# One-core hybrid block, Mamba stage: another order of VectorE's work in the odd tiles

## The chip, the cores and the metric

The kernel runs on one core of a Trainium2 chip. The metric is device time in microseconds (us) of one execution. The Mamba stage, in which the change lies, takes about 590 us of it.

## The reference

The kernel computes one block on 2 x 1024 rows of 512 elements, fp32, with a residual addition after each part:

```
x = x + attention(layernorm(x))      # sliding window, 16 heads
x = x + moe(layernorm(x))            # 8 experts, top 2
x = x + mamba(layernorm(x))
x = x + moe(layernorm(x))            # the same weights
```

The part that matters here is mamba (16 heads of 64, state 128, blocks of 64 rows, so two blocks in a tile of 128 rows):

```
z, xBC, dt_raw = split(x @ in_proj_w.T)            # 1024, 1280, 16 columns
xBC = silu(conv4(xBC) + conv_b)                    # 4 taps along the rows
dt = softplus(dt_raw + dt_bias);  A = -exp(A_log)
X = x_heads * dt;  A_disc = dt * A
Y = Y_diag + Y_off                                 # in a block, and from the state before it
Y = Y + x_heads * D
y = Y * silu(z);  y = y / rms(y) * norm_w
return y @ out_proj_w.T
```

## The kernel before

Four stages run one after the other: attention, the experts (moe_a), Mamba, the experts again (moe_b). Each engine has one instruction stream, written out by hand, and waits on semaphores. What an engine does next is set by the order of the calls in the code alone.

In the function mamba, 16 tiles of 128 rows are worked off in 8 turns of two tiles. A turn i scans tiles 2i (even) and 2i+1 (odd), and, in its first seven turns (front), prepares the two tiles of the next turn: it normalises their rows, multiplies them by in_proj_w, and convolves the 10 channel groups in five units (0 to 4) of two groups each, 256 rows wide. Of a unit TensorE makes the product (channels), ScalarE copies it into cin and makes the last tap (conv_in), VectorE adds the other three taps in six instructions (convolve, L1696), and ScalarE applies silu (conv_out, L1927).

For an odd tile VectorE does, in this order before the change: mask_products (L1731), scale_rows (L1737, waits for xs from ScalarE), keep_factors, convolve 1, mean_of, rest_of_y (L1711, the low half of the y of the tile before), convolve 2, mix (L1748, decays times cb), first_block (L1755, state in the middle of the tile), time_steps (L1660 to L1675, softplus by a series, 16 small instructions), second_block (L1762, state at the tile's end), convolve 3, put_out (L1725, the output with its residual, for the even tile t-1), scored.statistics (L201 to L204), own_out (L1772), scored.normalise (L215), convolve 4, rows_done (L1779, L1782, L1784) and logits_out (L246).

What the other engines need of it:

- TensorE: own_rows waits for mix and first_block; from_states (L2186) for second_block; scored.turn (L226) for scored.normalise; the turning of y (L2149) of the next tile for rows_done. Its order near the odd tile's end is own_rows, channels 4, from_states, gate_rows half 0 (L2119), scored.turn (L226), gate_rows half 1 (L2119), scored.product (L238), and then the next even tile: scan_rows (L2131 to L2136), turn_xs (L2142), turn_y (L2149).
- ScalarE: behind the exponentials (L1991) come conv_out 0, conv_out 1, conv_in 3, conv_out 2, conv_out 3, conv_in 4, conv_out 4, scored.turned_out (L232, which scored.product waits for), gate, and the next tile's exp table and small_out (L1947).
- GpSimd (step): xlast (L1592), mean_power (L1585), mid (L1602), xskip (L1606), and after first_block the product for the state (L1610), which second_block waits for.

```
                scored.turned_out(act, t - 1, bank[7])   # ScalarE, behind conv_out(n, 4, 1 - pp)
                gate_rows(t + 1, 0, 1, cin_ready, UNITS * n + 5)   # TensorE, behind scored.turn
                scored.product(pe, t - 1, bank[7])
```

Of the kernel before, what the change touches and what calls it, by code (L numbers as in the profile page):

```python
# [81 lines left out]
def after(eng, sem, n):  # L82

    if not isinstance(n, int) or n > 0:
        eng.wait_ge(sem, n)
# [15 lines left out]
def spread(ap, axis, n):  # L101

    v = ap.unsqueeze(axis)
    shape = list(v.shape)
    shape[axis] = n
    return v.broadcast_to(shape)
# [1287 lines left out]
def mamba(core, x_in, x_out, xn_rows, out_w, conv_w, conv_b, a_log, d_skip, dt_bias, norm_w):  # L1394
# [74 lines left out]
    with stage_semaphores(nc, "mam") as sem, ExitStack() as ctx:  # L1469
# [160 lines left out]
        def _(dve):  # L1630
            def statistics(link, n, par, turn):
                dve.wait_ge(x_loaded[par], 16 * turn + 16)
                link(nc.vector.bn_stats(st[:, par], x[:, par]))
                nc.vector.nop(nofuse=True)
                link(nc.vector.bn_aggr(mv[:, par], st[:, par]))
                nc.vector.tensor_scalar(var_eps[:, par:par + 1], mv[:, par, 1:2], EPS, None, ALU.add).then_inc(var_ready, 1)
# [20 lines left out]
            def time_steps(link, n, pp):  # L1657

                dve.wait_ge(e_mag_ready, n + 1)
                link(nc.vector.tensor_scalar(ratio, e_mag, 2.0, None, ALU.add))  # L1660
                link(nc.vector.reciprocal(ratio, ratio))
                link(nc.vector.tensor_tensor(ratio, e_mag, ratio, ALU.mult))
                link(nc.vector.tensor_tensor(ratio2, ratio, ratio, ALU.mult))
                link(nc.vector.tensor_scalar(series, ratio2, 1.0 / 15, None, ALU.mult))
                for odd in (13, 11, 9, 7, 5, 3):
                    link(nc.vector.scalar_tensor_tensor(out=series, in0=series, scalar=1.0 / odd, in1=ratio2,
                                                        op0=ALU.add, op1=ALU.mult))
                link(nc.vector.scalar_tensor_tensor(out=series, in0=series, scalar=1.0, in1=ratio,
                                                    op0=ALU.add, op1=ALU.mult))
                link(nc.vector.tensor_scalar(u, u, 0.0, None, ALU.max))  # L1670
                link(nc.vector.scalar_tensor_tensor(out=dt[:, pp], in0=series, scalar=2.0, in1=u,
                                                    op0=ALU.mult, op1=ALU.add))
                for par in range(2):
                    wide = da_wide[:, 2 * pp + par].rearrange("p (r s h) -> p r s h", r=REPS, s=2)
                    last = nc.vector.tensor_tensor(wide, spread(spread(dt[:, pp, par * H:par * H + H], 1, 2), 1, REPS),  # L1675
                                                   spread(a_pair, 1, REPS), ALU.mult)
                last.then_inc(da_ready, 1)

            def first_factor(i):

                return core.keep[:, i % TURNS_PER_BATCH:i % TURNS_PER_BATCH + 1]

            def halo_in(n):
                dve.wait_ge(cin_ready, UNITS * n)
                nc.vector.tensor_scalar(cin[:, :, 0:halo], cin[:, :, PAIR:PAIR + halo], first_factor(n), None, ALU.mult)\
                    .then_inc(halo_ready, 1)

            def convolve(link, n, unit):

                dve.wait_ge(cin_ready, UNITS * n + unit + 1)  # L1690
                if unit == 0:
                    after(dve, halo_ready, n)
                slot = conv[unit % 3]
                for k in range(halo):
                    for j, c in enumerate(units[unit]):
                        last = nc.vector.scalar_tensor_tensor(out=slot[:, j], in0=cin[:, c, k:k + PAIR],  # L1696
                                                              scalar=taps[:, c, k:k + 1], in1=slot[:, j],
                                                              op0=ALU.mult, op1=ALU.add)
                    if k < halo - 1:
                        link(last)  # L1700
                last.then_inc(conv_ready, 1)

            def mean_of(t):
                dve.wait_ge(squares_ready, t + 1)
                nc.vector.tensor_scalar(mean_eps, squares, 1.0 / INNER, EPS, ALU.mult, ALU.add).then_inc(mean_ready, 1)
# [22 lines left out]
            def mask_products(t):  # L1728
                dve.wait_ge(held_ready, t + 1)
                after(dve, mixed_ready, t)  # L1730
                nc.vector.tensor_tensor(cb, held[:, BC:BC + BLK], core.upto[:], ALU.mult).then_inc(cb_ready, 1)  # L1731

            def scale_rows(t, pp, par):
                dve.wait_ge(xs_ready, 2 * t + 2)
                after(dve, yd_made, 2 * t)
                after(dve, xlast_ready, t)
                nc.vector.tensor_tensor(by_head(xdt), by_head(xs), spread(dt[:, pp, par * H:par * H + H], 2, MHD), ALU.mult)\  # L1737
                    .then_inc(xdt_ready, 1)

            def keep_factors(t, keep):  # L1740
                dve.wait_ge(exps_ready, t + 1)
                after(dve, mid_decayed, t)
                nc.vector.tensor_scalar(kept, exps[:, KEPT:KEPT + H], keep, None, ALU.mult).then_inc(kept_ready, 1)
# [42 lines left out]
            def turn(link, i, pp, first=False, front=True):  # L1786
                n = i + 1
                t = 2 * i
                mask_products(t)
                scale_rows(t, pp, 0)  # L1790
                keep_factors(t, first_factor(i))
                if front:
                    halo_in(n)
                    for par in range(2):
                        statistics(link, t + 2 + par, par, n)
                if not first:
                    mean_of(t - 1)
                    rest_of_y(t - 1)
                if front:
                    for par in range(2):  # L1800
                        normalise(t + 2 + par, par)
                mix(t)
                first_block(t)
                second_block(t)
                if first:
                    rest_of_w_out()
                if not first:
                    put_out(t - 1)
                    dve.wait_ge(added, t)
                    scored.statistics(dve, link, xres)  # L1810
                if front:
                    for par in range(2):
                        rest_out(t + 2 + par, par)
                own_out(t)
                if not first:
                    dve.wait_ge(out_made, t)
                    scored.normalise(dve, t - 1, xres)
                rows_done(link, t, 0)
                if front:
                    magnitudes(link, n)  # L1820
                if front:
                    convolve(link, n, 0)
                if not first:
                    scored.logits_out(dve, t - 1, bank[7])
                t = 2 * i + 1
                mask_products(t)
                scale_rows(t, pp, 1)
                keep_factors(t, core.ones[:, 0:1])
                if front:
                    convolve(link, n, 1)  # L1830
                mean_of(t - 1)
                rest_of_y(t - 1)
                if front:
                    convolve(link, n, 2)
                mix(t)
                first_block(t)
                if front:
                    time_steps(link, n, 1 - pp)
                second_block(t)
                if front:  # L1840
                    convolve(link, n, 3)
                else:
                    dve.wait_ge(z_made, 2 * TILES)
                    sort.early_choice(link)
                put_out(t - 1)
                dve.wait_ge(added, t)
                scored.statistics(dve, link, xres)
                own_out(t)
                dve.wait_ge(out_made, t)
                scored.normalise(dve, t - 1, xres)  # L1850
                if front:
                    convolve(link, n, 4)
                rows_done(link, t, 1)
                scored.logits_out(dve, t - 1, bank[7])

            link = Chain(dve, chain)
# [18 lines left out]
            for i in range(TURNS):  # L1875
                turn(link, i, i % 2, first=(i == 0), front=(i < LAST))
# [486 lines left out]
```

## Time and profile before

| | us |
|---|---|
| runs, median of 3 | 1661.57 |
| runs, lowest and highest | 1661.12, 1667.22 |
| the profiled execution, its own time | 1657.97 |
| its span in the trace | 1656.3 |
| busy in the span: TensorE, VectorE, ScalarE, GpSimd | 1509.8, 927.4, 720.9, 596.1 |

The profiled execution lies 3.6 us below the median of the runs, and its span 1.67 us below its own time. Times in the trace are from the span's start. A row of the timeline is a run of like instructions on one engine: start, duration, what it is, how many, and in brackets the idle time before it and what ended that. The Mamba stage lies between about 750 and 1350 us.

### The profile page before, as it was taken

The page shows a single profiled execution, that of the slowest core. Times are in us where ns is not written, and L with a number is a line of the kernel's source. Part 1 is how long each engine was busy: PE and PEld are TensorE (multiplying, and loading weights), DVE is VectorE, ACT ScalarE, POOL GpSimd, SP SyncE. Part 2 cuts the span into 40 slices and gives each one's busy share as a digit, 9 for nine tenths or more (in the row PEclk, how much of TensorE's full clock was granted, in tenths as well). Part 3 has the DMA queues.
Part 4 walks back from the last instruction along what each step waited for, and adds up shares of the span by engine and source line. Part 5 has one row for each costly group of instructions (what it writes and reads, how often), then busy time and mean ns, then how long its engine had stood idle before and what let it go on. Part 6 is the DMA issues. An engine that isn't in the chain of part 4 may idle for free. (4 is left out here: it accounts for less than half of the span.)

```text
span 1656.3 us, 34129 instructions
## 1 busy us (share of the span) xinstructions
PE 1509.8 (91%) x11983; PEld 1267.9 (77%) x12004; DVE 927.4 (56%) x2133; ACT 720.9 (44%) x1784; POOL 596.1 (36%) x473
## 2 busy tenths in 40 slices
PE   6999999998699999978789999999999869999997
PEld 5788788787498889966668677777777648898896
DVE  4677777776622234215787786977878662222222
ACT  3666666666032234225454445554445302222222
POOL 5556556555223334430232222233222403333342
PEclk9999999999799999989899999999999979999999
DMA  5356455444589777432001101010010037787753
GB/s 211 117 184 207 143 183 204 160 163 160 200 274 320 204 229 195 84 61 75 14 20 33 39 27 40 20 33 23 34 37 21 20 140 249 209 265 199 185 91 56
DMA packets 95917, 212.36 MB, mean 128 GB/s; under 512 B 7216, under 2 KB 7216, under 8 KB 94512
## 3 DMA queue, kind: packets, MB, share of 16 engines
q1 hardware_dynamic: 76736, 166.58, 28.8%
q0 software_dynamic: 17472, 40.90, 12.4%
q10 hardware_dynamic: 1584, 3.15, 0.5%
q8 instruction: 86, 1.41, 0.3%
q14 instruction: 39, 0.32, 0.1%
HBM read 136.94 MB, written 73.66 MB: 127 GB/s over the span
## 5 line engine op out<-in xcount | busy, mean ns | idle before, releaser
L1298 PE MATMUL bank<-ring,halves 128*128 x1872 | 332.1, 326 | 3.5 <-ACT halves L1137 3.5
L1298 PEld LDWEIGHTS bank<-ring,halves 128*128 128x128 f32 x1872 | 303.0, 188 | 10.8 <-issue 4.5
L498 POOL TENSOR_TENSOR arena<-arena 128x1024 f32<-128x1024 f32 x64 | 123.8, 1934 | 142.1 <-DVE arena L578 140.6
L1696 DVE SCALAR_TENSOR_TENSOR arena<-arena 128x256 f32<-128x256 f32 x240 | 136.8, 612 | 17.8 <-ACT arena L1916 15.0
L1147 ACT ACTIVATE arena<-bank 128x512 f32<-128x512 f32 x78 | 46.7, 598 | 204.4 <-PE bank L1329 73.4
L1592 POOL TENSOR_TENSOR arena<-arena 128x1024 f32<-128x1024 f32 x16 | 31.3, 1958 | 273.6 <-ACT arena L1970 235.1
L791 PE MATMUL bank<-arena 128*128 128x128 f32 x1024 | 124.8, 281 | 1.8 <-ACT arena L691 0.8
L710 ACT ACTIVATE arena<-arena 128x256 f32<-128x256 f32 x256 | 126.2, 499 | 0.0
L791 PEld LDWEIGHTS bank<-arena 128*128 128x128 f32 x1024 | 118.8, 194 | 7.7 <-issue 3.6
L1117 POOL DMA_INDIRECT out_dram<-arena x39 | 61.8, 1584 | 153.4 <-issue 87.9
L1117 POOL DMA_INDIRECT mid_rows<-arena x39 | 61.8, 1585 | 151.7 <-issue 92.0
L1109 POOL DMA_INDIRECT arena<-normalised_rows,arena x78 | 79.4, 1018 | 99.3 <-PE bank L1281 47.6
L1137 ACT ACTIVATE halves<-bank 128x512 fp32r<-128x512 f32 x78 | 46.7, 598 | 147.1 <-PE bank L1281 147.0
L1186 DVE TENSOR_TENSOR moe_b_act_rest<-bank,moe_b_act_high 128x384 fp32r<-128x384 f32 x39 | 21.8, 558 | 152.3 <-ACT moe_b_act_high L1152 152.3
L2088 PE MATMUL bank<-halves,w_in_high 128*128 128x256 f32 x640 | 91.9, 286 | 1.6 <-DVE halves L1646 1.6
L1186 DVE TENSOR_TENSOR moe_a_act_rest<-bank,moe_a_act_high 128x384 fp32r<-128x384 f32 x39 | 21.7, 556 | 125.4 <-ACT moe_a_act_high L1152 125.4
L1927 ACT ACTIVATE arena<-arena 128x256 f32<-128x256 f32 x80 | 35.6, 501 | 115.3 <-DVE arena L1696 115.2
L2088 PEld LDWEIGHTS bank<-halves,w_in_high 128*128 128x128 f32 x640 | 80.9, 188 | 2.8 <-DVE halves L1646 1.8
L1191 DVE TENSOR_TENSOR halves<-bank,halves 128x512 fp32r<-128x512 f32 x78 | 53.9, 692 | 47.1 <-ACT halves L1137 47.0
L1180 DVE SCALAR_TENSOR_TENSOR arena<-arena,bank 128x352 f32<-128x352 f32 x78 | 45.2, 579 | 55.3 <-PE bank L1298 52.6
L2119 PE MATMUL bank<-w_in_high,halves 128*128 128x512 f32 x256 | 73.1, 431 | 1.0 <-ACT arena L1916 1.0
L831 PE MATMUL bank<-ident,arena 128*128 128x128 f32 x512 | 69.2, 279 | 2.7 <-POOL arena L498 2.7
(285 smaller groups left out, 3293.6 us busy)
## 6 DMA issues: line engine op xcount, KB each, us to landing
ring<-expert_halves SPq DMA_DIRECT2D x16, 4352.0 KB, 18.7
expert_halves<-expert_high SPq DMA_DIRECT2D x16, 1088.0 KB, 8.4
expert_halves<-expert_rest SPq DMA_DIRECT2D x16, 1088.0 KB, 10.5
arena<-in_w_dram SPq DMA_DIRECT2D x8, 1088.0 KB, 6.7
normalised_rows<-arena SPq DMA_DIRECT2D x33, 256.0 KB, 2.0
arena<-in_x_dram SPq DMA_DIRECT2D x32, 256.0 KB, 2.8
arena<-mid_rows SPq DMA_DIRECT2D x32, 256.0 KB, 2.8
w_in_raw<-in_in_w_dram SPq DMA_DIRECT2D x16, 290.0 KB, 7.1
```

What stands on the lines that cost most here:

```text
L498: nc.gpsimd.tensor_tensor(held, held, spread(rinv[:, HG * g:HG * g + HG], 2, 2 * P), ALU.mult)\
L710: last = nc.scalar.activation(held, held, ACT.Exp, scale=-1.0, bias=nmax[:, h:h + 1], accum_out=psum_p[:, h:h + 1])
L791: last = nc.tensor.matmul(proj[:, c * P:c * P + P], wqkv[:, k, first + c * P:first + c * P + P], xnT[:, k], start=(k == 0), stop=(k == KD ...
L831: last = nc.tensor.transpose(b[:, j * P:j * P + P], probs[:, g // 2, HG * (g % 2) + 2 * half + j // 2, (j % 2) * P:(j % 2 + 1) * P], core. ...
L1109: nc.gpsimd.indirect_dma_start(out=rows[:, s % 2], out_offset=None, in_=xn_rows, in_offset=bass.IndirectOffsetOnAxis(ap=index[:, s:s + 1], ...
L1117: nc.gpsimd.indirect_dma_start(out=x_rows, out_offset=bass.IndirectOffsetOnAxis(ap=index[:, s:s + 1], axis=0), in_=y[:, s % 2], in_offset= ...
L1137: nc.scalar.activation(rows_parts[0][:, par], bank[0][:], ACT.Copy).then_inc(rows_high, 1)
L1191: nc.vector.tensor_tensor(rows_parts[1][:, par], bank[0][:], rows_parts[0][:, par], ALU.subtract)\
L1298: last = nc.tensor.matmul(bank[1 + 2 * par + part][:, 0:INTER], rows_parts[a][:, par, k * P:k * P + P], weights(at, b, (2 * k + part) * IN ...
L1696: last = nc.vector.scalar_tensor_tensor(out=slot[:, j], in0=cin[:, c, k:k + PAIR], scalar=taps[:, c, k:k + 1], in1=slot[:, j], op0=ALU.mul ...
L2088: last = nc.tensor.matmul(unit_banks[unit][:, j * PAIR:(j + 1) * PAIR], w_parts[b][:, k, at:at + P], x_parts[a][:, k], start=((a, b, k) == ...
L2119: last = nc.tensor.matmul(b_out[:], x_parts[a][:, k, par * P:par * P + P], w_parts[b][:, k, half * 512:half * 512 + 512], start=((a, b, k) ...
```

## The change

In the odd tile's part of VectorE's turn, mix and first_block are called ahead of convolve 2, and time_steps moves from behind first_block to behind scored.normalise, so that second_block, convolve 3, put_out, the statistics, own_out and normalise all run ahead of it. Nothing is added or removed, and no other engine's stream changes. It takes effect where front holds, in seven of the eight odd tiles; in the last one the order is as before.

```diff
--- before.py
+++ after.py
@@ -1830,12 +1830,10 @@
                     convolve(link, n, 1)
                 mean_of(t - 1)
                 rest_of_y(t - 1)
-                if front:
-                    convolve(link, n, 2)
                 mix(t)
                 first_block(t)
                 if front:
-                    time_steps(link, n, 1 - pp)
+                    convolve(link, n, 2)
                 second_block(t)
                 if front:
                     convolve(link, n, 3)
@@ -1849,6 +1847,7 @@
                 dve.wait_ge(out_made, t)
                 scored.normalise(dve, t - 1, xres)
                 if front:
+                    time_steps(link, n, 1 - pp)
                     convolve(link, n, 4)
                 rows_done(link, t, 1)
                 scored.logits_out(dve, t - 1, bank[7])
```

VectorE's stream at the beginning of that part, before (L1711 is rest_of_y, L1696 convolve 2, L1748 mix, L1755 first_block, L1660 the first of time_steps):

```order
L1711 TENSOR_TENSOR mam_yT_rest<-bank,mam_yT_high 128x512 x2
L1696 SCALAR_TENSOR_TENSOR arena<-arena 128x256 x6
L1748 TENSOR_TENSOR arena<-arena 128x1024
L1755 TENSOR_TENSOR arena<-arena,bank 128x512 x2
L1660 TENSOR_SCALAR arena<-arena 128x32
L1661 RECIPROCAL arena<-arena 128x32
L1662 TENSOR_TENSOR arena<-arena 128x32
```

and in the changed kernel:

```order
L1711 TENSOR_TENSOR mam_yT_rest<-bank,mam_yT_high 128x512 x2
L1748 TENSOR_TENSOR arena<-arena 128x1024
L1755 TENSOR_TENSOR arena<-arena,bank 128x512 x2
L1696 SCALAR_TENSOR_TENSOR arena<-arena 128x256 x6
L1762 TENSOR_TENSOR arena<-arena,bank 128x512 x2
L1696 SCALAR_TENSOR_TENSOR arena<-arena 128x256 x6
```

Mix and first_block have gone past the six instructions of unit 2, and second_block (L1762) follows unit 2 directly. The end of the same part, from second_block to unit 4 (L1725 is put_out, L201 to L204 the statistics, L1772 own_out, L215 normalise), before:

```order
L1762 TENSOR_TENSOR arena<-arena,bank 128x512 x2
L1696 SCALAR_TENSOR_TENSOR arena<-arena 128x256 x6
L1725 SCALAR_TENSOR_TENSOR arena<-bank,arena 128x512
L201 BN_STATS arena<-arena 128x6
L203 BN_AGGR arena<-arena 128x2
L204 TENSOR_SCALAR arena<-arena 128x1
L1772 TENSOR_TENSOR arena<-arena,bank 128x512 x2
L215 TENSOR_SCALAR arena<-arena 128x512
L1696 SCALAR_TENSOR_TENSOR arena<-arena 128x256 x6
```

and in the changed kernel, from own_out to the end of the series, behind which unit 4 follows:

```order
L1772 TENSOR_TENSOR arena<-arena,bank 128x512 x2
L215 TENSOR_SCALAR arena<-arena 128x512
L1660 TENSOR_SCALAR arena<-arena 128x32
L1661 RECIPROCAL arena<-arena 128x32
L1662 TENSOR_TENSOR arena<-arena 128x32
L1663 TENSOR_TENSOR arena<-arena 128x32
L1664 TENSOR_SCALAR arena<-arena 128x32
L1666 SCALAR_TENSOR_TENSOR arena<-arena 128x32 x6
L1668 SCALAR_TENSOR_TENSOR arena<-arena 128x32
L1670 TENSOR_SCALAR arena<-arena 128x32
L1671 SCALAR_TENSOR_TENSOR arena<-arena 128x32
L1675 TENSOR_TENSOR arena<-arena 128x128 x2
```

Before, normalise and unit 4 stood next to each other; now the series (L1660 to L1675) lies between them, and no longer ahead of second_block.

## Rows read from the trace of the kernel before

**Rows 1.** The page, part 2: granted TensorE clock in 40 slices of the span

```profile
PEclk9999999999799999989899999999999979999999
```

**Rows 2.** Busy time by engine in a turn: us, PE, PEld, DVE, ACT, POOL, clock, DMA

```profile
1000.00:1072.00 72.00, 67.35 (x633) 53.94 (x634) 54.83 (x107) 36.88 (x95) 19.66 (x14) 1.00 0.09 31
```

**Rows 3.** Timeline of VectorE in the odd tile of turn 2

```profile
965.11 1.23 DVE L1737 TENSOR_TENSOR arena<-arena 128x1024 f32<-128x1024 f32 x1 [0.75 <-ACT arena L1954]
...
971.92 5.54 DVE L1696 SCALAR_TENSOR_TENSOR arena<-arena 128x256 f32<-128x256 f32 x6
977.38 1.22 DVE L1748 TENSOR_TENSOR arena<-arena 128x1024 f32<-128x1024 f32 x1
...
980.31 1.51 DVE L1662 TENSOR_TENSOR arena<-arena 128x32 f32<-128x32 f32 x1
981.86 0.19 DVE L1663 TENSOR_TENSOR arena<-arena 128x32 f32<-128x32 f32 x1
...
984.74 1.28 DVE L1762 TENSOR_TENSOR arena<-arena,bank 128x512 f32<-128x512 f32 x2
...
991.74 0.54 DVE L215 TENSOR_SCALAR arena<-arena 128x512 f32<-128x512 f32 x1
992.19 2.71 DVE L1696 SCALAR_TENSOR_TENSOR arena<-arena 128x256 f32<-128x256 f32 x6
```

**Rows 4.** Timeline of GpSimd in the same odd tile

```profile
971.40 1.90 POOL L1602 TENSOR_TENSOR arena<-arena 128x1024 f32<-128x1024 f32 x1
973.26 2.09 POOL L1606 TENSOR_TENSOR arena<-arena 128x1024 f32<-128x1024 f32 x1
979.88 1.90 POOL L1610 TENSOR_TENSOR arena<-arena 128x1024 f32<-128x1024 f32 x1 [4.53 <-DVE arena L1755]
```

**Rows 5.** Timelines of VectorE and GpSimd in the next even tile

```profile
1009.36 1.24 DVE L1748 TENSOR_TENSOR arena<-arena 128x1024 f32<-128x1024 f32 x1 [1.60 <-ACT arena L1991]
...
1009.48 2.88 POOL L1606 TENSOR_TENSOR arena<-arena 128x1024 f32<-128x1024 f32 x1
```

**Rows 6.** Timeline of TensorE at the odd tile's end, turns 2 and 3

```profile
985.48 1.94 PE L2186 MATMUL bank<-arena 128*64 128x512 f32 x8 [0.34 <-DVE arena L1762]
...
989.31 1.09 PE L2119 MATMUL bank<-w_in_rest,halves 128*128 128x512 f32 x4
992.33 0.91 PE L226 MATMUL bank<-ident,arena 128*128 128x128 f32 x4 [1.93 <-DVE arena L215]
992.89 3.52 PE L2119 MATMUL bank<-w_in_high,halves 128*128 128x512 f32 x8
...
1063.06 2.10 PE L2119 MATMUL bank<-w_in_high,halves 128*128 128x512 f32 x8
...
1066.70 1.06 PE L238 MATMUL bank<-gate,arena 128*128 128x8 f32 x8 [0.60 <-ACT arena L232]
```

**Rows 7.** Timeline of ScalarE at the odd tile's end, turn 2

```profile
994.93 0.91 ACT L1927 ACTIVATE arena<-arena 128x256 f32<-128x256 f32 x2 [4.14 <-DVE arena L1696]
995.75 0.58 ACT L232 ACTIVATE arena<-bank 128x512 f32<-128x512 f32 x1
```

**Rows 8.** Two of five stretches at half clock; columns as in rows 2

```profile
927.74:931.15 3.41, 3.41 (x17) 3.39 (x16) 0.92 (x2) 1.71 (x5) 0.00 (x0) 0.50 0.00 0
992.59:996.00 3.41, 3.41 (x11) 2.76 (x10) 3.34 (x8) 1.06 (x3) 0.00 (x0) 0.50 0.47 154
```

**Rows 9.** Timeline of VectorE: where five tiles begin (scale_rows)

```profile
893.79 1.23 DVE L1737 TENSOR_TENSOR arena<-arena 128x1024 f32<-128x1024 f32 x1 [0.75 <-ACT arena L1954]
...
930.45 1.23 DVE L1737 TENSOR_TENSOR arena<-arena 128x1024 f32<-128x1024 f32 x1 [2.08 <-ACT arena L1954]
...
1001.77 1.23 DVE L1737 TENSOR_TENSOR arena<-arena 128x1024 f32<-128x1024 f32 x1 [1.38 <-ACT arena L1954]
...
1035.43 1.23 DVE L1737 TENSOR_TENSOR arena<-arena 128x1024 f32<-128x1024 f32 x1 [0.75 <-ACT arena L1954]
...
1071.39 1.23 DVE L1737 TENSOR_TENSOR arena<-arena 128x1024 f32<-128x1024 f32 x1 [1.38 <-ACT arena L1954]
```

## The prediction

> **What bounds the kernel now.** I read the busy time of a turn first. In 72 us, a turn and a little, TensorE is busy 67.35 us and VectorE 54.83 [rows 2], so TensorE sets the pace wherever it is not waiting, and the change can only give time where TensorE waits for something that VectorE does in an odd tile. I then looked for these waits in TensorE's timeline. There are three late in an odd tile: 0.34 us ahead of from_states (L2186), ended by second_block (L1762); 1.93 us ahead of the turning of the normalised rows (L226), ended by normalise (L215); and in turn 3 another 0.60 us ahead of the scores' product (L238), ended by ScalarE's L232 [rows 6]. The last is VectorE too: L232 stands right behind the silu of unit 4 (L1927), which sat idle 4.14 us for VectorE's L1696 and L232 began as soon as it was done [rows 7].
>
> Then VectorE's timeline of that tile, to see what it is late with. From scale_rows at 965.11 to the end of unit 4 at 992.19 + 2.71 = 994.90 are 29.79 us [rows 3], and it never waits in between: VectorE is the path here. Of these, some time is not work. Six instructions of unit 2 took 5.54 us while those of unit 4 took 2.71; one 32-column product (L1662) took 1.51 where its neighbour of the same shape (L1663) took 0.19 [rows 3]. In just these stretches GpSimd was in its 1024-column products: L1602 and L1606 from 971.40 to 975.35, L1610 from 979.88 to 981.78 [rows 4]. So an instruction of VectorE with both inputs in SBUF stands still until GpSimd's is over: 5.54 - 2.71 = 2.83 and 1.51 - 0.19 = 1.32, together 4.15 us on the path.
>
> Last, the clock. Most slices have it at 9 tenths or more [rows 1]. In the seven odd tiles with front it fell to half, 1.2 instead of 2.4 GHz, five times, for 3.41 us each. Three of these falls came right behind the 1.93 us idle, as at 992.59; two, the one at 927.74 among them, behind the idle at the end of the tile and the small matmuls of the product and of scan_rows [rows 8]. Their price is in the distances between tiles [rows 9], with the odd tile's start from [rows 3]. An odd tile without a fall takes 1071.39 - 1035.43 = 35.96 us, one with a fall at its gate_rows 1001.77 - 965.11 = 36.66: 0.70. The fall at 927.74 cost 930.45 - 893.79 = 36.66, again 0.70, and in the following even tile 34.66 instead of 33.66, another 1.00: 1.70, since there TensorE has nothing to wait for and all is paid. The profiled execution paid 3 x 0.70 + 2 x 1.70 = 5.5 us.
>
> **The change, part by part.** No instruction is added or removed. I follow the odd tile of turn 2 in us behind scale_rows.
>
> *Mix and first_block ahead of unit 2.* Mix could start at 6.9, where unit 2 did. GpSimd's L1602 is then running until 8.19 [rows 4], so mix is held and ends at about 9.3 instead of 8.05: 1.25 lost. xskip (L1606) waits for mix in turn. The even tile shows that order: mix from 1009.36 to 1010.60, L1606 stretched to 2.88 us and over 1.76 behind mix [rows 5]; so here it ends at 11.05. First_block reads a bank of PSUM, and instructions of that kind were not stretched; it runs from 9.2 to 10.5. Its sums release GpSimd's L1610, now at 11.1 instead of 14.77.
>
> *Unit 2 behind them.* Its first instruction meets the end of L1606 (0.33 lost) and its second all of L1610: 1.64, since now, too, of the 2.83 lost to two products about 1.2 go to the rest of the first and 1.6 to the whole of the second. Unit 2 takes 4.7 us, to 15.2. Held in all: 1.25 + 0.33 + 1.64 = 3.22 instead of 4.15, since L1662 meets no GpSimd product any more. That is 0.93 gained on VectorE's path. Bounds: if none of the three holds came, 4.15; if unit 2 met both of GpSimd's products as it does now, and mix too, 4.08 held, 0.07 gained. I take 0.93, because every hold has its like in the rows.
>
> *Second_block earlier.* It ends at 16.4, not 20.9. From_states then waits for TensorE alone: the 0.34 goes, and gate_rows half 0 ends at 25.29 - 0.31 = 24.98 [rows 6].
>
> *Normalise ahead of the series.* The series took 5.0 us with its hold; without it normalise ends at 22.5 instead of 27.17 [rows 3]. TensorE comes to L226 at 24.98, so the 1.93 is gone. It goes on with gate_rows half 1 at 25.54 and, at full clock (3.04 us between L2119 at 1063.06 and the end of its work at 1066.10), is ready for the product at 28.6.
>
> *What is late next.* Unit 4 comes after the series and still has all of VectorE's work ahead of it. It ends at 29.79 - 0.93 = 28.86. The silu of unit 4 and L232 take 1.48 us to release the product: before (turn 3) the product began at 1066.70 - 1035.43 = 31.27 [rows 6, 9], 1.48 behind unit 4's 29.79; now at 30.34. TensorE so waits 30.34 - 28.6 = 1.8 us at the product instead of 1.93 and 0.60 at two places. The turn gives back 0.93, not 2.9: the wait is moved, not removed. Seven turns: 6.5 us. The time steps' own consumer, scan_rows, wants them after the product at 31; they end at 26.3, so moving them costs nothing; if they came 5 us later they would.
>
> *The clock.* The wait at the product is followed by the product with 8 columns and scan_rows with 16, the very stretch behind which the two dear falls came, and those with only 0.60 idle ahead of it. With 1.8 there I count a fall in six of the seven turns, at 1.70, and none any more at L226: 10.2 us instead of 5.5, 4.7 lost. Bounds: two falls as now (3.4) and seven (11.9).
>
> **The sum:** -6.5 + 4.7 = -1.8 us, on the profiled execution 1657.97 - 1.8 = 1656.2, and as that lay 3.6 us below the median of the runs, 1659.8 as a median.
>
> Against this stands a rule of the Trainium skill ("TensorE: Matmul & The Clock Gate", "Why this matters for your kernels"): to keep the clock it asks only that idle gaps between bursts be avoided which are longer than any that TensorE has here in a turn. By it no turn would lose the clock, and the change would bring the first rival's time. The trace disagrees, with falls behind 1.93 and near 0.60 us of idle.
>
> **Rivals.**
>
> 1. *The clock stays up.* The long idle is gone from L226, and if the product and scan_rows hold the clock, the falls end: for it speaks that in turns 3 and 5 the same stretch passed without one. With no falls -6.5 - 5.5 = -12.0, 1649.6; with as many as now -6.5, 1655.1. Over 0.5% faster (8.3 us) needs at most two.
>
> 2. *The holds are not saved.* GpSimd's products are the same in number, and unit 2 and mix may meet all. With 0.07 per turn and seven falls: -0.5 + 6.4 = +5.9, 1667.5. For it speaks only that who starts first decides, by tenths of a us; against it, that all odd tiles look alike.
>
> 3. *Slower: two falls in a row.* If the clock stays at half for twice 3.41 us because small matmuls at half clock follow the idle, each turn pays 3.4: 23.8 - 5.5 - 6.5 = +11.8, 1673.4. It passes the 0.5% when the falls cost over (8.3 + 12.0) / 7 = 2.9 us per turn. Against it: all five falls ended after one stretch.
>
> **How the numbers follow.** Forecast 0.56, rival 1 0.22, rival 2 0.14, rival 3 0.08. A measurement of this kernel tells about 0.5%, 8.3 us, from no change. Faster by more than that: most of rival 1, 0.18. Slower: rival 3 and a scrap of rival 2, 0.09. The same: 0.73. The range leaves out rival 3 and the ends of rivals 1 and 2: 1652.0 to 1666.0. The forecast's own range, four to seven falls and 0.7 to 1.2 us saved per turn, is 1655 to 1662. The likeliest is 1659.8.
>
> **What the profile would show.** Right: no idle ahead of L226 in odd tiles of turns 0 to 6, near 1.8 us ahead of L238; L1662 at 0.19 us; mix at 2.4; unit 4 ending 28.9 us behind scale_rows; an odd tile of 35.0 us without a fall; half clock about the product and the next tile's transposes in nearly all turns. Wrong: a product that follows gate_rows at once, or a clock that stays at full speed over these stretches (then 1 holds), or mix and unit 2 held over 4 us together (then 2).

## The result: slower, and the profile after

The changed kernel takes 1674.25 us (median of 9 runs, 1666.62 to 1677.04), the kernel before beside it 1661.12 (9 runs). The ratio is 1.0082, with a 95% interval of 1.0059 to 1.0105. Forecast were 1659.8 us and no measurable change. The profiled execution took 1674.25, its span is 1672.5, 16.2 us more than before. Between the start of the first odd tile and that of the last even one, the stretch of the seven changed tiles, are 12.4 us of it; the rest is 1.8 us in the tile behind the last changed one and 2 us outside.

The page (part 1's line and the clock of part 2, to be held against [rows 1]) and the sum over that stretch:

```profile
PE 1528.3 (91%) x11983; PEld 1286.2 (77%) x12004; DVE 924.8 (55%) x2133; ACT 721.2 (43%) x1784; POOL 597.4 (36%) x473
...
PEclk8999999999799999989889999999998979999999
```

```profile
823.59:1295.10 471.51, 443.17 (x3983) 358.93 (x3996) 357.55 (x693) 230.29 (x585) 127.35 (x90) 0.94 0.09 29
```

TensorE is busy longer for the same matmuls, and its clock over the stretch is 0.94. In the kernel before the same stretch was 459.12 us at 0.98:

```profile
822.54:1281.66 459.12, 429.35 (x3986) 342.95 (x3999) 359.60 (x693) 230.19 (x585) 124.83 (x90) 0.98 0.09 29
```

VectorE and GpSimd in the odd tile of turn 4, which begins at 1113.04 (timelines, as [rows 3, 4]):

```profile
1120.00 2.31 DVE L1748 TENSOR_TENSOR arena<-arena 128x1024 f32<-128x1024 f32 x1
1122.24 1.27 DVE L1755 TENSOR_TENSOR arena<-arena,bank 128x512 f32<-128x512 f32 x2
1123.43 4.82 DVE L1696 SCALAR_TENSOR_TENSOR arena<-arena 128x256 f32<-128x256 f32 x6
1128.17 1.28 DVE L1762 TENSOR_TENSOR arena<-arena,bank 128x512 f32<-128x512 f32 x2
...
1135.17 0.54 DVE L215 TENSOR_SCALAR arena<-arena 128x512 f32<-128x512 f32 x1
...
1136.22 0.19 DVE L1662 TENSOR_TENSOR arena<-arena 128x32 f32<-128x32 f32 x1
...
1139.34 2.71 DVE L1696 SCALAR_TENSOR_TENSOR arena<-arena 128x256 f32<-128x256 f32 x6
```

```profile
1119.34 1.90 POOL L1602 TENSOR_TENSOR arena<-arena 128x1024 f32<-128x1024 f32 x1
1121.19 2.89 POOL L1606 TENSOR_TENSOR arena<-arena 128x1024 f32<-128x1024 f32 x1
1124.05 2.08 POOL L1610 TENSOR_TENSOR arena<-arena 128x1024 f32<-128x1024 f32 x1
```

Mix is held for GpSimd's L1602 and takes 2.31 us, L1606 waits for it in turn (2.89), unit 2 takes 4.82, L1662 is at 0.19 again, and normalise ends at 1135.71, 22.67 us behind scale_rows. Unit 4 ends at 29.00 instead of 29.79. The holds come to 1.09 us in mix and 2.11 in unit 2, 3.20 in all for a forecast 3.22.

TensorE at the end of that tile, and ScalarE beside it (timelines, as [rows 6, 7]; lines behind the change have moved up by one, L2118 was L2119, L2141 was L2142):

```profile
1137.60 0.60 PE L226 MATMUL bank<-ident,arena 128*128 128x128 f32 x4
1137.95 2.09 PE L2118 MATMUL bank<-w_in_high,halves 128*128 128x512 f32 x8
1139.89 1.09 PE L2118 MATMUL bank<-w_in_rest,halves 128*128 128x512 f32 x4
1143.52 1.49 PE L238 MATMUL bank<-gate,arena 128*128 128x8 f32 x8 [2.54 <-ACT arena L232]
1144.86 0.45 PE L2130 MATMUL bank<-ident,arena 128*128 128x128 f32 x1
1145.10 0.63 PE L2131 MATMUL bank<-upto_own,arena 128*128 128x128 f32 x2
1145.53 0.45 PE L2133 MATMUL bank<-arena,upto_own 128*128 128x16 f32 x2
1145.82 0.59 PE L2133 MATMUL bank<-arena,past_own 128*128 128x16 f32 x2
1146.24 1.01 PE L2133 MATMUL bank<-arena,in_block 128*128 128x16 f32 x4
1147.19 0.48 PE L2135 MATMUL bank<-arena 128*64 128x64 f32 x4
1147.60 1.97 PE L2141 MATMUL bank<-ident,arena 128*128 128x128 f32 x8
1149.36 1.74 PE L2148 MATMUL bank<-ident,arena 128*128 128x128 f32 x8
```

```profile
1142.08 0.91 ACT L1926 ACTIVATE arena<-arena 128x256 f32<-128x256 f32 x2 [7.80 <-DVE arena L1696]
1142.89 0.57 ACT L232 ACTIVATE arena<-bank 128x512 f32<-128x512 f32 x1
...
1147.72 0.49 ACT L1946 ACTIVATE arena<-bank 128x384 f32<-128x384 f32 x1 [1.76 <-PE bank L2135]
```

The 1.93 us ahead of L226 are gone; 2.54 us stand ahead of the product, which comes 30.48 us behind scale_rows. Behind it everything is slow: turn_xs (L2141) takes 1.97 us and turn_y (L2148) 1.74, and ScalarE waits 1.76 us for scan_rows. The granted clock in stretches laid on it (columns as in [rows 2]) tells why:

```profile
1143.97:1147.38 3.41, 3.41 (x21) 3.37 (x20) 1.83 (x3) 1.95 (x3) 0.00 (x0) 0.50 0.02 5
1147.38:1150.80 3.42, 3.42 (x19) 3.30 (x18) 0.30 (x2) 1.69 (x4) 0.00 (x0) 0.50 0.00 0
1150.80:1154.20 3.40, 3.33 (x16) 2.33 (x15) 3.15 (x8) 2.15 (x5) 0.77 (x1) 1.00 0.01 2
```

Half speed, 1.2 GHz, for two stretches of 3.41 us on end. The clock falls in all seven turns, for 6.83 us in five of them and for 10.24 in the first and the last. Before, it was five of seven, 3.41 us each [rows 8].

### The profile page after: what moved, and what is told of

Its sections match the earlier page's. It is cut to its first block and busy times, and to the rows that moved or that the text cites. A ratio compares the mean times of both kernels' runs of the same rounds, so it can differ in the third digit from the quotient of the medians.

```text
span 1672.5 us, 34129 instructions
## 1 busy us (share of the span) xinstructions
PE 1528.3 (91%) x11983; PEld 1286.2 (77%) x12004; DVE 924.8 (55%) x2133; ACT 721.2 (43%) x1784; POOL 597.4 (36%) x473
## 3 DMA queue, kind: packets, MB, share of 16 engines
q0 software_dynamic: 17472, 40.90, 12.4%
## 5 line engine op out<-in xcount | busy, mean ns | idle before, releaser
L1696 DVE SCALAR_TENSOR_TENSOR arena<-arena 128x256 f32<-128x256 f32 x240 | 131.7, 590 | 17.8 <-ACT arena L1915 15.0
L2118 PE MATMUL bank<-w_in_high,halves 128*128 128x512 f32 x256 | 72.1, 427 | 1.0 <-ACT arena L1915 1.0
```

Of the source, the lines that this page charges most:

```text
L2118: last = nc.tensor.matmul(b_out[:], x_parts[a][:, k, par * P:par * P + P], w_parts[b][:, k, half * 512:half * 512 + 512], start=((a, b, k) ...
```

## The experiments

Each kernel was timed beside the kernel before; ratios are to that one, with 95% intervals. The kernel before took 1661.12 us beside the changed kernel, 1657.32 beside e1 to e4, 1658.30 beside e5 to e8, 1657.65 beside e9 to e11 and 1657.26 beside e12, so kernels of different groups are compared by their ratios. "Stretches" counts the 3.41 us pieces at half clock between the starts of tiles 1 and 14 in the one profiled execution; idle is TensorE's in a changed odd tile, in us. In the kernel before, the 0.60 us come only in the four turns whose clock has not fallen behind L226.

| kernel | idle ahead of L226 | ahead of the product | stretches | median us | ratio |
|---|---|---|---|---|---|
| before | 1.93 | 0.60 | 5 | | 1 |
| changed | 0 | 2.53 | 16 | 1674.25 | 1.0082 (1.0059 to 1.0105) |
| e1 changed, filled | 0 | 0.35 | 3 | 1651.29 | 0.9960 (0.9940 to 0.9979) |
| e2 mix and first_block alone | 1.70 | 0.60 | 2 | 1653.38 | 0.9970 (0.9951 to 0.9990) |
| e3 series alone | 0 | 3.91 | 21 | 1692.46 | 1.0213 (1.0184 to 1.0241) |
| e4 series behind unit 4 | 0 | 0 | 6 | 1645.25 | 0.9926 (0.9898 to 0.9953) |
| e5 before, filled | 0.19 | 0.15 | 2 | 1661.84 | 1.0015 (0.9996 to 1.0035) |
| e6 changed, half filled | 0 | 1.45 | 9 | 1663.69 | 1.0026 (1.0002 to 1.0050) |
| e7 as e4, filled | 0 | 0 | 0 | 1641.23 | 0.9887 (0.9861 to 0.9912) |
| e8 changed, L232 ahead | 0 | 0 | 1 | 1643.72 | 0.9904 (0.9879 to 0.9929) |
| e9 before, filled further | 0.19 | 0.15 | 0 | 1659.77 | 1.0012 (0.9987 to 1.0037) |
| e10 as e8, filled | 0 | 0 | 0 | 1642.33 | 0.9905 (0.9880 to 0.9931) |
| e11 before, L232 ahead | 1.94 | 0 | 2 | 1647.95 | 0.9937 (0.9915 to 0.9959) |
| e12 before, filled wholly | 0 | 0 | 0 | 1655.33 | 0.9994 (0.9976 to 1.0012) |

The stretches are counted in one execution of each kernel. The mean granted clock of every execution says the same of the others: 0.961 to 0.971 in the 83 executions of the kernel before beside the experiments, 0.952 to 0.959 in the 9 of the changed kernel, 0.967 to 0.974 in the 12 of e1, 0.947 to 0.952 in the 6 of e3. In e6, where it varies from 0.958 to 0.968, the execution with the highest clock is the fastest (1655.05 us) and the one with the lowest the slowest (1671.37).

The theory (A) was that the joined idle ahead of the product, which small matmuls follow, makes the clock fall for longer, and that this is the whole loss. The rivals were that the wait, the moved holds, or the series' place cost by themselves.

**e1: the idle filled.** All waits stay, TensorE only does something in one of them: stay_busy issues ten dummy matmuls (L179, 512 columns, bf16) whose results nobody reads.

```diff
                     gate_rows(t + 1, 0, 1, cin_ready, UNITS * n + 5)
+                    pe.wait_ge(own_ready, 2 * t + 2)
+                    stay_busy(core, bank[5], 10)
                 scored.product(pe, t - 1, bank[7])
```

> The changed kernel with ten dummy matmuls of 512 columns (bf16, into bank 5, which is free then) ahead of the scores' product in odd tiles, where TensorE now idles 2.53 us. Theory A (the clock): in the changed kernel TensorE's clock falls to half behind that idle in all seven turns, for 6.83 us or more; with the idle filled it does not, an odd tile takes 35.2 us and an even one 33.7, and the Mamba stage loses 23 to 25 us against the changed kernel: about 1650, 0.6% below the kernel before. Theory B (the wait itself, or VectorE's order, is the loss): dummies change no wait, so the time stays at 1670 to 1676.

Measured: 1651.29 us, a ratio of 0.9960 against the changed kernel's 1.0082. The same stretch of tiles, an odd tile and an even one of it, and TensorE at the tile's end (sum over a window and two timelines of e1):

```profile
823.74:1275.11 451.37, 437.74 (x4046) 345.93 (x4066) 352.63 (x693) 230.15 (x585) 131.47 (x90) 0.99 0.09 30
```

```profile
1102.25 1.23 DVE L1737 TENSOR_TENSOR arena<-arena 128x1024 f32<-128x1024 f32 x1 [0.75 <-ACT arena L1953]
...
1137.39 1.23 DVE L1737 TENSOR_TENSOR arena<-arena 128x1024 f32<-128x1024 f32 x1 [1.38 <-ACT arena L1953]
...
1171.05 1.22 DVE L1737 TENSOR_TENSOR arena<-arena 128x1024 f32<-128x1024 f32 x1 [0.75 <-ACT arena L1953]
```

```profile
1130.25 2.11 PE L179 MATMUL bank<-att_mask,onesb 128*128 128x512 bf16 x9
1132.70 1.06 PE L238 MATMUL bank<-gate,arena 128*128 128x8 f32 x8 [0.35 <-ACT arena L232]
...
1135.14 1.09 PE L2141 MATMUL bank<-ident,arena 128*128 128x128 f32 x8
1136.07 1.04 PE L2148 MATMUL bank<-ident,arena 128*128 128x128 f32 x8
```

451.37 instead of 471.51 us at a clock of 0.99. The product comes no sooner, 30.45 us behind scale_rows; but turn_xs (L2141) is at 1.09 us again. An odd tile takes 35.14 us and an even one 33.66. Theory B is out: with every wait in place, an odd tile without a fall is 0.82 us shorter than before (35.96); what the change costs is the clock behind the wait. With these two lengths, seven odd and six even tiles without any fall make 447.9 us, so the falls cost the changed kernel (471.5 - 447.9) / 7 = 3.4 us a turn.

**e2 and e3: the halves of the change.** In e2 the series stays ahead of second_block and mix and first_block go ahead of unit 2; in e3 unit 2 stays where it was and the series goes behind normalise. Both edits are shown against the changed kernel.

```diff
                 mix(t)
                 first_block(t)
                 if front:
                     convolve(link, n, 2)
+                    time_steps(link, n, 1 - pp)
                 second_block(t)
...
                 if front:
-                    time_steps(link, n, 1 - pp)
                     convolve(link, n, 4)
```

> Only the first half of the change: mix and first_block ahead of unit 2; the series stays behind them and ahead of second_block. Theory A (the clock): VectorE's path is 0.8 us shorter as in the changed kernel, but the idle stays split, about 1.5 us ahead of the turning of the normalised rows (L226) and 0.6 ahead of the product, so the clock falls no oftener than before: 1653 to 1657. Theory B (the moved holds of mix are the loss): slower than before, 1665 or more.

```diff
-                mix(t)
-                first_block(t)
                 if front:
                     convolve(link, n, 2)
+                mix(t)
+                first_block(t)
                 second_block(t)
```

> Only the second half: unit 2 stays ahead of mix, the series goes behind normalise. Second_block then follows first_block at once and must wait about 2.0 us for GpSimd's state product, which the series used to cover, while the series no longer is held 1.3 us: unit 4 ends 0.7 us later than before. Theory A: the idle ahead of the product is 3 us or more and the clock falls each turn for two stretches: 1680 to 1688, slower than the whole change. Theory B (the series' place costs nothing by itself): 1661 to 1668.

Measured: e2 1653.38, 0.3% faster than before; e3 1692.46, slower than the whole change, and slower than theory A had said by 4 us. TensorE at the end of an odd tile in e2, then VectorE at second_block and TensorE at the product in e3 (timelines):

```profile
1126.77 0.66 PE L226 MATMUL bank<-ident,arena 128*128 128x128 f32 x4 [1.71 <-DVE arena L215]
...
1130.82 1.06 PE L238 MATMUL bank<-gate,arena 128*128 128x8 f32 x8 [0.60 <-ACT arena L232]
```

```profile
1142.72 1.28 DVE L1762 TENSOR_TENSOR arena<-arena,bank 128x512 f32<-128x512 f32 x2 [2.01 <-POOL arena L1610]
```

```profile
1158.06 1.87 PE L238 MATMUL bank<-gate,arena 128*128 128x8 f32 x8 [3.91 <-ACT arena L232]
```

In e2 the idle stays split, 1.71 and 0.60 us. VectorE gains its 0.8 us (unit 4 ends at 28.98), and only two turns lose the clock. In e3 second_block waits 2.01 us for GpSimd, since nothing covers its product any more; the product's wait grows to 3.91 us, and the clock is down for three stretches in every turn. So the half of the change that helps is the first; the series' move, by emptying the wait at L226 into the one at the product, undoes it.

**e4: the series behind unit 4.** One step further the same way, which lets unit 4 go first.

```diff
                 if front:
-                    time_steps(link, n, 1 - pp)
                     convolve(link, n, 4)
+                    time_steps(link, n, 1 - pp)
```

> The changed kernel with the series one step later still, behind unit 4 instead of ahead of it. Unit 4 then ends about 25.2 us behind scale_rows instead of 29.0, the product follows gate_rows without a wait, scan_rows comes 2 to 3 us earlier, waiting a few tenths for the series, and TensorE waits next for y, about 1 us. Theory A: the turn is 1.8 to 3 us shorter than one without falls before, and at most single falls come: 1645 to 1656. Theory B (VectorE's total work bounds the odd tile, whatever its order): the same as the changed kernel less its double falls at best, not under 1655.

Measured: 1645.25, in theory A's range. TensorE at the end of an odd tile (timeline), and the clock behind it:

```profile
1128.70 0.95 PE L238 MATMUL bank<-gate,arena 128*128 128x8 f32 x8
1130.02 0.30 PE L2130 MATMUL bank<-ident,arena 128*128 128x128 f32 x1 [0.36 <-issue]
...
1131.27 0.45 PE L2135 MATMUL bank<-arena 128*64 128x64 f32 x4
1131.65 1.97 PE L2141 MATMUL bank<-ident,arena 128*128 128x128 f32 x8
1133.69 1.59 PE L2148 MATMUL bank<-ident,arena 128*128 128x128 f32 x8
```

```profile
1131.34:1134.75 3.41, 3.34 (x18) 2.82 (x18) 2.47 (x4) 1.58 (x4) 0.00 (x0) 0.50 0.02 5
```

Unit 4 ends at 25.3 us and the product stands right behind gate_rows. Scan_rows starts 0.36 us behind it; the view names no releaser, but the series ended at 1129.91, 0.11 us ahead of scan_rows. Yet six of seven turns have one fall, with no idle but those 0.36 us between the small matmuls of the product and of scan_rows. So a fall needs no long idle here.

**e6: half of the idle filled,** five dummies instead of ten in e1's edit.

> The changed kernel with five dummy matmuls ahead of the product instead of ten: about 1.45 of the 2.53 us stay idle. If the number of half-clock stretches follows the length of the idle, one stretch of 3.41 us instead of two comes in most turns, at 1.66 us each: 7 x 1.66 = 11.6 us above the full filling, 1660 to 1665. If any idle above 1 us costs as much as 2.5, it stays near the changed kernel, 1670; if only idle near 2 us costs, it is as the full filling, 1651.

Measured: 1663.69, in the forecast interval, but not in the forecast way. Four turns on end had two stretches each, the next two none, the last one. The idle was 1.42 to 1.45 us in all seven, so the number of stretches does not follow its length alone; what else decides it is open.

**e7: e4 with its idle and small matmuls filled.**

```diff
                 scan_rows(t, pp, 0)
+                if begun:
+                    pe.wait_ge(own_ready, 2 * t)
+                    stay_busy(core, bank[5], 4)
...
+                    pe.wait_ge(own_ready, 2 * t + 2)
+                    stay_busy(core, bank[5], 2)
                 scored.product(pe, t - 1, bank[7])
```

> The kernel with the series behind unit 4, with two dummies ahead of the product and four between scan_rows and turn_xs. There TensorE waits for y in any case, and six of seven turns still had one fall. Theory A: they vanish, turns take 66.5 us instead of 68.3, 9 to 11 us less: 1633 to 1638. Theory B (the falls there are hidden behind the wait for y, or the dummies cost what they save): 1643 to 1648.

Measured: 1641.23 and no fall in the turns, 4.0 us under e4 where 9 to 11 were expected. An odd and an even tile take 33.68 + 34.14 = 67.8 us, not 66.5, against 33.83 + 34.44 in e4: its falls had lain in good part beside the wait for y, and cost 0.45 us a turn. In e4 the turning of y (L2148) began at 1133.69, 0.05 us behind the end of L1784 which it needs, so turn_xs at half clock had cost it next to nothing.

**e8 and e11: ScalarE's order instead.** The product waits for L232, and L232 for the silu of unit 4 only by its place. e8 is this edit on the changed kernel, e11 on the kernel before.

```diff
                     conv_in(n, 4)
+                    scored.turned_out(act, t - 1, bank[7])
                     conv_out(n, 4, 1 - pp)
-                scored.turned_out(act, t - 1, bank[7])
+                else:
+                    scored.turned_out(act, t - 1, bank[7])
```

> The changed kernel with ScalarE's stream altered instead of TensorE's or VectorE's: scored.turned_out (L232) stands ahead of conv_out 4. VectorE's order is that of the change, the series ahead of unit 4. If the wait at the product comes only from L232 standing behind unit 4's silu, the product follows gate_rows at once, the 2.53 us idle goes and TensorE waits next for y, about 1.5 us: 1643 to 1652, with a single fall in most turns. If the order on ScalarE is not what matters, 1670.

> The kernel before with only ScalarE's stream altered (L232 ahead of conv_out 4), VectorE's order untouched. It tells what VectorE's new order is worth once nothing joins the waits: the product follows gate_rows without its 0.60 us, but the 1.93 us ahead of L226 stay, since normalise is as late as before. Falls about as before. Expected 4 us (7 x 0.6) below the kernel before, 1652 to 1656, and 9 to 12 us above the changed kernel with the same alteration (1643.7). If instead VectorE's new order is worth nothing, both come out alike at 1644.

Measured: e8 1643.72, e11 1647.95. In e8 (timeline) the product follows gate_rows (L2120) at once, and TensorE's next wait is the one for y:

```profile
1052.81 1.09 PE L2120 MATMUL bank<-w_in_rest,halves 128*128 128x512 f32 x4
1053.74 0.95 PE L238 MATMUL bank<-gate,arena 128*128 128x8 f32 x8
...
1058.71 1.09 PE L2150 MATMUL bank<-ident,arena 128*128 128x128 f32 x8 [1.36 <-DVE arena L1784]
```

VectorE's order is the same in e8 and in the changed kernel, and 1.8% lie between them (0.9904 and 1.0082), some 30 us. E11 is 9.7 us under the kernel before, where 4 had been expected: its product comes at 30.51 us instead of 31.27 in the turns without a fall, and only two turns lose the clock. With L232 ahead in both, the change of VectorE's order brings 1647.95 down to 1643.72, less than the 9 to 12 us expected, and the two intervals overlap. In the profiles an odd tile without a fall takes 33.80 us in e8 and 35.09 in e11, an even one 34.00 and 33.66: 7 x 1.29 - 6 x 0.34 = 7.0 us, so some of the gain is given back in the even tile.

**e10: e8 with five dummies between scan_rows and turn_xs.**

> The changed kernel with L232 ahead of conv_out 4 and five dummies between scan_rows and turn_xs, where TensorE waits 1.4 us for y. That profile had one fall in the turns, its median was 1643.7 against a profiled 1640.5, so some executions have more. With the wait filled none should come: 1638 to 1642. If the clock no longer matters here, 1643 to 1645.

Measured: 1642.33, no fall in the turns. This is 0.3 us above the one forecast and 0.7 below the other, and not to be told from e8, so it settles neither.

**e5, e9, e12: the idle of the kernel before filled.** Eight and two dummies (e5), two more behind scan_rows (e9), nine and three (e12).

```diff
                     gate_rows(t + 1, 0, 0, cin_ready, UNITS * n + 4)
+                    pe.wait_ge(added, t)
+                    stay_busy(core, bank[7], 8)
                 scored.turn(pe, t - 1, bank[7])
```

> The kernel before with its two idle places in odd tiles filled: eight dummy matmuls ahead of the turning of the normalised rows (1.93 us idle), two ahead of the product (0.60). Theory A (the clock is paid for idle of either place): the falls between tiles vanish, the profiled kernel before paid 5.5 us for them, so 0.3 to 0.5% below the kernel before, and 3 to 7 us above the changed kernel with its idle filled, which is VectorE's 0.8 us a turn. Theory B (only the joined, long idle of the changed kernel costs): no change from the kernel before.

> The kernel before with both idle places filled as in the earlier run, and two more dummies between scan_rows and turn_xs, ahead of which there is no idle in this kernel, so that they cost 0.43 us a turn, 2.6 us in all. The earlier filling brought nothing in the median though its profile showed only two falls in the turns. If falls in other executions come from the small matmuls of the product and scan_rows alone, which the earlier dummies did not break up, these two end them and the time drops to 1653 to 1657 and varies less. If not, it is the earlier filling plus 2.6: 1661 to 1666.

> The kernel before with nine and three dummies, so that less than 0.1 us stays idle at either place (eight and two left 0.19 and 0.15). The first filling brought nothing in the median, 1661.84, though its profiled execution, with two falls in the turns, was its fastest at 1654.19. If the falls in its other executions came from the idle that was left, the median now drops to 1652 to 1655. If filling these places does not change how often the clock falls in the kernel before, it stays at 1657 to 1662, and the profile shows falls between tiles whose number goes with its time.

Measured: 1661.84, 1659.77 and 1655.33; none can be told from the kernel before. For e5 theory A had said 0.3 to 0.5% less, and that did not come; e9 lies between its two forecasts and e12 0.3 us above its first. In e12's profile there is no fall in the turns and 453.6 us for the stretch that took 459.1. Over its 12 executions the mean granted clock is 0.968, against 0.9655 for the 17 of the kernel before beside it, which is about 9 us less at half clock, an estimate of two to three stretches. At 1.1 us each (5.5 us for five) they would be worth some 3 us; the ratio's interval, 4 us faster to 2 us slower, holds these 3 us as well as none. So what the falls cost the kernel before in an average execution is not known. The medians of e5 and e12, two dummies a turn apart, differ by 6.5 us, but their ratios, 1.0015 and 0.9994, have intervals that overlap.

E12 and e1 are the two orders of VectorE with their idle filled: ratios 0.9994 and 0.9960, 0.34% or some 5.6 us apart, with intervals that just overlap. The traces give 7 x (35.96 - 35.14) = 5.7 us. That is what the change is worth with the clock set aside, near the 6.5 us that the forecast had for it.

## Why the prediction was wrong

**VectorE's path: right.** Forecast was 0.93 us saved per odd tile by fewer holds; 0.79 were measured (29.79 to 29.00), with mix at 2.31 us for 2.4 and unit 2 at 4.82 for 4.7. Mix ended 1.07 us behind the end of GpSimd's L1602, while first_block, with one input in PSUM, took its 1.27 us beside L1606. The trace agrees with the Trainium skill here ("SBUF — State Buffer", "Who interferes with whom"): the ports that VectorE and GpSimd share are an exclusive lock, for which a VectorE instruction with two inputs in SBUF contends with a GpSimd one that reads SBUF, and one with a single input in SBUF does not.

**The wait at L226, and what is late next: right in place, low in size.** The 1.93 us went, the product came at 30.48 for a forecast 30.34. But TensorE was ready at 27.9, not 28.6, so it idled 2.53 us and not 1.8. L226 came at 24.56, not 24.98: I had overlooked that own_rows (L2209) no longer waits for first_block, so that it began at 14.76 and not at 14.94 as in the kernel before and in e3, and had counted to the modelled end of gate_rows, where the next matmul starts 0.16 us ahead of such an end. Another 0.21 us came from L226 itself, which I had read in a turn where the clock fell in the midst of it: gate_rows half 1 started 0.35 us behind it instead of 0.56.

**The clock: the step that failed.** It is the sentence "With 1.8 there I count a fall in six of the seven turns, at 1.70". Seven turns fell, for two stretches on end and twice for three, at 3.4 us a turn. The term was put at 10.2 us and was 23.6 against turns without falls. With the forecast's 5.5 us for the kernel before, the sum is -5.5 (7 x 0.79) + 23.6 - 5.5 = +12.6 us; the traces of the stretch differ by 12.4. I had taken the price from falls that an idle of 0.60 us preceded [rows 8, 9], and held two stretches in a row for unlikely because none of five had been longer. But none of these five had a long idle directly ahead of the small matmuls, which is what the change makes. And I had looked at the seven turns alone. Elsewhere in the same trace of the kernel before, ten of the thirteen falls that ended within it lasted 6.83 or 10.24 us. One of them stood behind the product of the last odd tile, which the change leaves as it is, with waits of 0.86 and 1.17 us inside it (timeline, and stretches laid on the fall):

```profile
1327.57 0.65 PE L226 MATMUL bank<-ident,arena 128*128 128x128 f32 x4 [1.77 <-DVE arena L215]
1328.91 1.06 PE L238 MATMUL bank<-gate,arena 128*128 128x8 f32 x8 [0.69 <-ACT arena L232]
```

```profile
1330.51:1333.92 3.41, 1.97 (x8) 1.57 (x8) 2.03 (x7) 0.63 (x2) 0.00 (x0) 0.50 0.00 0
1333.92:1337.33 3.41, 2.91 (x7) 2.33 (x8) 1.82 (x4) 1.49 (x3) 0.55 (x1) 0.50 0.00 0
```

Rival 3 named just this, with 1673.4 us, and was given 0.08. E1 shows that the clock behind the idle is the cause and no wait. E2 and e3 show that it is the series' move that brings it about, though in e3 second_block's wait of 2.01 us adds to the idle. Why two stretches come here and three there is not shown.

**The rule on idle gaps.** In the changed kernel all seven turns lost the clock behind 2.53 us of idle, and in e4 six did behind 0.36 us. The rule of the Trainium skill ("TensorE: Matmul & The Clock Gate", "Why this matters for your kernels") asks to avoid idle gaps over about 3 us between bursts of matmuls; by it no turn would have lost the clock, so the traces contradict it here.

**Rivals 1 and 2** fell: the clock did not stay up, and 0.95 us of holds were saved a turn (3.20 left of 4.15).

## What to carry to other kernels

When an edit takes away one of two waits of TensorE, ask where the same time will be idle instead: two waits of 1.93 and 0.60 us joined into one of 2.53 us, ahead of matmuls of 8 and 16 columns, brought falls of the clock that cost 3.4 us a turn. Find the engine whose order joins them; here one ScalarE instruction standing behind another for no reason of data was worth some 30 us on the changed kernel. And take the price and the length of a fall from all falls of the trace, the longest among them, not from the few places that the change touches.

## What the runs showed of the hardware

- With a wait of 2.53 us ahead of small matmuls the clock was at half for 6.83 us in five turns and 10.24 in two; with 3.91 us of wait, 10.24 in all seven (e3).
- In the changed kernel the last six falls came 71.68 us from each other, while the products came 72.0 us apart; in e4 all six came 68.27 us from each other, in e3 all seven 75.09. No run shows why.
- In all seven changed odd tiles GpSimd's 1.90 us product L1606, issued while VectorE's mix was still waiting for the product before it, let mix go first and took 2.89 us from issue.
- In the profiled execution of the kernel before one fall cost 1.1 us on average (5.5 us for five); in e4, where TensorE's next step needed VectorE in any case, it was 0.45 us a turn against e7.
